# Expert weights spread by DMA, silu in PSUM, and t as the stationary block of the down projection

## The reference

```python
probs = softmax(x @ gate_w)                     # 1024 x 32
w, sel = top_k(probs, 8);  w = w / sum(w)
# an expert takes its first C = 512 tokens, the others are dropped
g = einsum('ech,ehi->eci', xg, w_gate)          # 256 -> 96, each expert
u = einsum('ech,ehi->eci', xg, w_up)
y = einsum('eci,eih->ech', silu(g) * u, w_down) # 96 -> 256
out[token] += w_slot * y
```

## Time and profile before

| | |
|---|---|
| median of 3 runs | 268.94 us (268.77 to 269.79) |
| the profiled execution | 269.13 us |
| its span | 266.8 us |
| mean granted TensorE clock | 0.976 of 2.4 GHz |
| first gate projection starts | 35.8 us |
| second half starts | about 158.6 us |
| last down matmul starts | about 261.0 us |

### The profile page before, as it was taken

The page is one execution under the profiler, slowest core; times in us unless marked ns, Lnnn a source line. Parts: engine busy times, 40 slices in busy tenths (PEclk is TensorE's granted clock), DMA queues, the critical chain, the costliest instruction groups (busy, mean ns, idle before and its releaser), DMA issues.

```text
span 266.8 us, 3968 instructions
## 1 busy us (share of the span) xinstructions
PE 243.9 (91%) x1058; PEld 186.9 (70%) x1061; DVE 134.8 (51%) x342; ACT 134.3 (50%) x242; POOL 161.1 (60%) x140
## 2 busy tenths in 40 slices
PE   6636798799999999999999999999999999999993
PEld 1412486677678777778687778787878787878772
DVE  4598887339562794439643534235342332424333
ACT  2766453576366753594377635343525353435320
POOL 5118202856768565858586675858677686868610
PEclk9999879799999999999999999999999999999998
DMA  7950500006050524124050505050505060700002
GB/s 208 258 147 22 156 26 0 0 0 185 16 154 22 135 64 121 56 50 127 10 169 6 173 1 161 17 153 26 156 21 166 13 173 17 222 22 0 1 0 79
DMA packets 43359, 22.23 MB, mean 83 GB/s; under 512 B 34128, under 2 KB 43344, under 8 KB 43344
## 3 DMA queue, kind: packets, MB, share of 16 engines
q1 hardware_dynamic: 42496, 21.63, 28.1%
q10 hardware_dynamic: 848, 0.43, 0.6%
HBM read 21.01 MB, written 1.05 MB: 83 GB/s over the span
## 4 chain that ended last, share of the span: by engine, by line
PE 68%; DVE 14%; ACT 6%; issue 6%; POOL 4%; DMA 1%; DVEq 0%; POOLq 0%; ACTq 0%
PE bank L699 40%; PE bank L717 8%; PE bank L721 7%; PE bank L718 7%; DVE t_sb L1042 3%; DVE bank L911 2%; DVE inv L922 2%; POOL rstd L357 2%; DVE t_sb L1048 2%; PE bank L616 2%; PE bank L657 2%; PE bank L706 1%; ACT normed L446 1%; DMA x_sb<-in_x_dram 1%; POOL t_lo L375 1%
## 5 line engine op out<-in xcount | busy, mean ns | idle before, releaser
L375 POOL TENSOR_TENSOR t_lo<-t_sb,t_hi 128x512 fp32r<-128x512 f32 x47 | 60.8, 1294 | 75.1 <-ACT t_hi L542 75.1
L349 POOL TENSOR_TENSOR wlo<-raw,whi 128x768 fp32r<-128x768 f32 x48 | 88.5, 1847 | 6.7 <-ACT whi L505 6.5
L699 PE MATMUL bank<-h_hi,whi 128*128 128x512 f32 x192 | 80.8, 421 | 0.3 <-issue 0.3
L1042 DVE TENSOR_TENSOR t_sb<-bank,s_sb 128x512 f32<-128x512 f32 x48 | 33.1, 690 | 93.4 <-PE bank L706 45.8
L699 PE MATMUL bank<-h_lo,whi 128*128 128x512 f32 x192 | 76.7, 400 | 0.0
L699 PE MATMUL bank<-h_hi,wlo 128*128 128x512 f32 x192 | 76.2, 397 | 0.0
L542 ACT ACTIVATE t_hi<-t_sb 128x512 fp32r<-128x512 f32 x48 | 30.3, 630 | 90.9 <-DVE t_sb L1048 90.9
L505 ACT ACTIVATE whi<-raw 128x768 fp32r<-128x768 f32 x48 | 40.0, 835 | 8.6 <-PE bank L721 8.6
L699 PEld LDWEIGHTS bank<-h_hi,whi 128*128 128x128 f32 x192 | 36.9, 192 | 8.8 <-issue 0.8
L699 PEld LDWEIGHTS bank<-h_hi,wlo 128*128 128x128 f32 x192 | 36.6, 191 | 8.8
L699 PEld LDWEIGHTS bank<-h_lo,whi 128*128 128x128 f32 x192 | 36.8, 192 | 8.0
(11 more groups left out here) (120 smaller groups left out, 194.0 us busy)
## 6 DMA issues: line engine op xcount, KB each, us to landing
raw<-in_L_ffn_w_gate_dram SPq DMA_DIRECT2D x16, 384.0 KB
raw<-in_L_ffn_w_up_dram SPq DMA_DIRECT2D x16, 384.0 KB
raw<-in_L_ffn_w_down_dram SPq DMA_DIRECT2D x48, 128.0 KB
out_dram<-x SPq DMA_DIRECT2D x4, 256.0 KB, 2.5
x_sb<-in_x_dram SPq DMA_DIRECT2D x1, 512.0 KB, 7.0
ctx_tile<-in_ctx_dram SPq DMA_DIRECT2D x4, 128.0 KB, 5.2
x_sb<-in_x_dram SPq DMA_DIRECT2D x1, 256.0 KB, 3.4
ctx_sb<-in_ctx_dram SPq DMA_DIRECT2D x1, 256.0 KB, 4.6
```

What stands on the lines that cost most here:

```text
L349: pool.tensor_tensor(split_view(wlo, slot, part), raw_parts(slot, part), split_view(whi, slot, part).bitcast(F32), ALU.subtract).then_inc( ...
L375: pool.tensor_tensor(t_lo[k % 2][:], t_sb[:], t_hi[k % 2][:].bitcast(F32), ALU.subtract).then_inc(t_lo_ready, 1)
L699: last = nc.tensor.matmul(ps[:], up_weight(w, slot, part, k, j), h[:, k, tokens], start=(i == 0), stop=(i == len(terms) - 1))
L1042: nc.vector.tensor_tensor(t1_sb[:], w_ps[:], s_sb[:], ALU.mult).then_inc(t1_ready, 1)
```

## The change

- The routing weights are no longer split into bf16 parts. They are turned as float32 (`turn_chosen`), copied to `route` (32 rows, float32), and for each group SP issues a DMA from SBUF to SBUF (`spread`) that writes the four experts' rows 32 times each into `w_sb[slot]`. DVE waits for its landing (`w_landed`).
- SP's program is written out without loops, with the spreadings in between. The contexts of `later(4)` and `later(5)` are loaded behind reload(4) and reload(6).
- silu is written over g in its PSUM bank; g and u go over a ring of four banks; a projection waits for t1 or t of two steps back.
- In `down`, 128 tokens of t are the stationary block and 256 columns of w_down move: 12 matmuls in place of 6. y comes out with tokens on the partitions, so the copy and the transposes at the end of a half go, and DVE adds straight from the two banks. The first two tiles are signalled (`y_ready`) before the last two.
- Removed: the tables `expert3` and `spread`, `take_y`, `turn_output`, the weights matmul.

```diff
-        ring = (bank[2], bank[3], bank[6])
+        ring = (bank[2], bank[3], bank[6], bank[4])
...
+            def load(n):
+                slot, group = n % 2, n % GROUPS
...
+            def reload(n):
+                sp.wait_ge(w_hi_ready, (n - 1) * 3)
+                sp.wait_ge(w_lo_ready, (n - 1) * 3)
+                load(n)
+            def spread(n):
+                half, group, slot = n // GROUPS, n % GROUPS, n % 2
+                sp.wait_ge(route_ready, ROUTED if half else 2)
+                if n >= 2:
+                    sp.wait_ge(t1_ready, (n - 1) * GT + 1)
+                rows = route[group * EG:(group + 1) * EG, None, half * HALF:(half + 1) * HALF]
+                sp.dma_start(w_sb[slot][:], rows.to_broadcast([EG, QI, HALF])).then_inc(w_landed[slot], 16)
...
+            load(0)
+            load(1)
+            load_context(3)
+            reload(2)
+            spread(0)
+            for n in range(1, 2 * GROUPS):
+                spread(n)
+                if n + 2 < 2 * GROUPS:
+                    reload(n + 2)
+                if n in (2, 4):
+                    load_context(n // 2 + 3)
...
             for u in first_routed:
                 route_exps(u)
+            take_route(first_routed[0])
...
-                nc.scalar.activation(s_sb[:], g_ps(k)[:], ACT.Silu).then_inc(s_ready, 1)
+                nc.scalar.activation(g_ps(k)[:], g_ps(k)[:], ACT.Silu).then_inc(s_ready, 1)
...
-                if part == 0 and (not isinstance(n, int) or n >= 2):
-                    pe.wait_ge(t_ready, n)
-                elif part == 1 and (not isinstance(n, int) or n >= 1):
-                    pe.wait_ge(s_ready, n)
+                if not isinstance(n, int) or n >= 2:
+                    pe.wait_ge((t1_ready, t_ready)[part], n)
...
-                for m in range(KT):
-                    nc.tensor.matmul(y_ps[m][:], down_weight(whi, slot, j, m), t_hi[odd][:], start=False, stop=False)
-                    nc.tensor.matmul(y_ps[m][:], down_weight(wlo, slot, j, m), t_hi[odd][:], start=False, stop=False)
+                def product(t, a, b, stop=False):
+                    return nc.tensor.matmul(y_tile(t), a[odd][:, t * P:(t + 1) * P], down_weight(b, slot, j), start=False, stop=stop)
+                for t in range(HT):
+                    product(t, t_hi, whi)
+                    product(t, t_hi, wlo)
                 pe.wait_ge(t_lo_ready, n + 2)
-                for m in range(KT):
-                    last = nc.tensor.matmul(y_ps[m][:], down_weight(whi, slot, j, m), t_lo[odd][:],
-                                            start=False, stop=last_step)
+                for t in range(HT):
+                    last = product(t, t_lo, whi, last_step and t % NT == NT - 1)
+                    if last_step and t == NT - 1:
+                        last.then_inc(y_ready, 1)
                 last.then_inc(down_done, 1)
...
             project(0, 0, 0, 0, 0, 0)
+            turn_chosen(first_routed[0])
             project(0, 0, 1, 0, 0, 0)
+            turn_chosen(first_routed[1])
             project(1, 0, 0, 0, 1, 0)
-            for u in first_routed:
-                turn_parts(u)
...
-                dve.wait_ge(w_turned, group + 1)
+                dve.wait_ge(w_landed[slot], spreads * 16)
                 dve.wait_ge(s_ready, n + 1)
                 dve.wait_ge(t_ready, n + 1)
-                nc.vector.tensor_tensor(t1_sb[:], w_ps[:], s_sb[:], ALU.mult).then_inc(t1_ready, 1)
+                nc.vector.tensor_tensor(t1_sb[:], g_ps(k)[:], w_sb[slot][:], ALU.mult).then_inc(t1_ready, 1)
...
+                    for t in range(q * NT, (q + 1) * NT):
+                        rows = x1[:, half * HT + t, :]
+                        last = nc.vector.tensor_tensor(rows, rows, y_tile(t), ALU.add)
```

More of the change, by code:

```diff
@@ L161, in program @@
         wlo = [sb(f"wlo{i}", [P, 3, PART], F32R) for i in range(2)]
-        s_sb = sb("s_sb", [P, HALF])
+        w_sb = [sb(f"w_sb{i}", [P, HALF]) for i in range(2)]
         t1_sb = sb("t1_sb", [P, HALF])
@@ L279, in _ @@
             sp.dma_start(x_sb[:, HT:, :], xt[:, HT:, :]).then_inc(x_landed[2], 16)
-            def load(slot, group):
-                experts = bass.ds(group * EG, EG)
+            def load(n):
+                slot, group = n % 2, n % GROUPS
+                experts = slice(group * EG, (group + 1) * EG)
                 for part, w in ((0, wg_dram), (1, wu_dram)):
@@ L287, in load @@
                     sp.dma_start(raw[slot][:, 2, j * C:(j + 1) * C], wd_dram[experts, :, j, :]).then_inc(raw_landed[slot], 16)
-            sp.dma_start(ctx_tile[:], ct[:, HT:HT + 1, :]).then_inc(tile_landed, 16)
-            load(0, 0)
-            load(1, 1)
+            def reload(n):
[9 more added lines that the diff above has]
+                sp.dma_start(w_sb[slot][:], rows.to_broadcast([EG, QI, HALF])).then_inc(w_landed[slot], 16)
             def load_context(n):
                 sp.wait_ge(v_turned, n)
[L295 to L312, removed]
+                sp.dma_start(ctx_tile[:], ct[:, n + 2:n + 3, :]).then_inc(tile_landed, 16)
+            sp.dma_start(ctx_tile[:], ct[:, HT:HT + 1, :]).then_inc(tile_landed, 16)
+            load(0)
[9 more added lines that the diff above has]
+                    load_context(n // 2 + 3)
             for quarter in range(4):
@@ L338, in _ @@
                                pattern=[[1, P]], channel_multiplier=-1)
-            for part in range(3):
-                chain.link(pool.affine_select(out=expert3[:], in_=expert3[:], compare_op=ALU.not_equal, fill=1.0,
-                                              base=-part * E, pattern=[[-1, E]], channel_multiplier=1))
             pool.memset(neg_half[:], -0.5).then_inc(consts_ready, 1)
@@ L572, in turn @@
                         split_high(ahead % 2, k % GT, it * 2 + (half * GROUPS + ahead))
-            def take_y(half):
-                act.wait_ge(down_done, (half + 1) * STEPS + 2)
-                if half:
-                    act.wait_ge(y_turned, 2)
-                for q in range(2):
-                    cols = slice(q * NT * P, (q + 1) * NT * P)
-                    nc.scalar.activation(y_sb[:, 0, cols], y_ps[0][:, cols], ACT.Copy).then_inc(y_copied[0], 1)
             turn(0, 0, later(3), early, early_routed, first_turn=True)
@@ L701, in project @@
                 last.then_inc(ready, 1)
-            def weights(n, half, group):
-                pe.wait_ge(t1_ready, n + 1)
-                nc.tensor.matmul(w_ps[:], spread[:].rearrange("p e i -> p (e i)")[:, bass.ds(group * P, P)],
-                                 route[:, half * HALF:(half + 1) * HALF], start=True, stop=True).then_inc(w_turned, 1)
             def down(n, slot, j, odd, group, last_step=False):
@@ L753, in turn @@
                     if half or not first_turn or k:
-                        project(n, half, 1, slot, j, it * 2 + (half * GROUPS + slot))
-                    if first_turn and k == 0:
-                        pe.wait_ge(route_ready, ROUTED if half else 2)
-                        if half == 0:
-                            pe.wait_ge(tables_ready, 1)
-                    if j == 0:
-                        weights(n, half, it * 2 + slot)
+                        project(n, half, 1, slot, k, it * 2 + (half * GROUPS + slot))
                     if half == 0 and first_turn and k == 0:
@@ L1057, in turn @@
                 for k in range(TURN_STEPS):
-                    step(it * TURN_STEPS + (half * STEPS + k), k, it * 2 + (half * GROUPS + k // GT))
+                    step(it * TURN_STEPS + (half * STEPS + k), k, it + (half * TURNS + 1))
                     for stage, u in beside.get(k, []):
```

135 lines of the change are left out of this document (50 added, 85 removed).

## The result

The changed kernel takes **308.13 us** (median of 4 runs, 307.79 to 309.72), the kernel before 269.37 us beside it (268.77 to 269.84): ratio **1.1452 [1.1402, 1.1502]**. I had forecast 279.0 and a range of 269 to 285: the sign was right, the size was off by 29 us, and the range did not hold it. The profiled execution has a span of 306.6 us, 39.8 more than before. Single executions of one and the same kernel can be slow by one to two per cent: the ratios and their intervals leave these out, the medians count them.

A forecast was written before the change was run, and what follows sets the result against it. TensorE, busy 91% of the span, was taken as the bound. Terms -3.5 + 5.9 + 5.2 + 1.6 + 3.0 - 0.9 - 1.4 = +9.9 us on 269.13 gave 279.0 us, range 269.0 to 285.0.

The forecast's parts named there:

- The first step: Start of step 0: the first spreading lands at 46.0, so t1 starts 3.0 us later, +3.0 us; bounds +1.3 and +5.5.
- The later spreadings: Spreadings of later groups: hidden under a whole group of matmuls while they land in time, so 0 us.
- my bound of 7 us: Upper bound for the first spreading, the longest load's 7 us, which would make the first step +5.5 us.
- more waiting: Rival: two falls of the clock and spreadings late in the groups too, 282 to 290 us; chance 0.12.
- the cover of a group: Second half: a group's matmuls, 12.9 us, hide the later spreading; packets twice as slow would use this up.
- Weights matmul: Steps on TensorE: removing the matmul that makes the routing weights saves 15 x 0.2325, -3.5 us.
- Down: Down projection: 12 matmuls of 256 columns at 0.1265 us replace 6 of 512 at 0.2325, +5.9 us.
- Half price: Rival on down: 256-column matmuls cost half of the 512 price, 0.1165 us, giving 273.2 us; chance 0.14.
- the output: Middle loses 8 transposes on TensorE, -0.9 us; at the end additions start at the half-way signal, -1.4 us.
- Context: Second and third turn: context tile is issued later, so TensorE waits 2.8 and 2.4 us, +5.2; bounds 0 and 8.
- one clock fall: After the two context stalls: TensorE drops once to the 1.2 GHz level, +1.6 us; bounds 0 and +3.2.
- Ring and silu in PSUM: Projections wait on t1 or t of two steps back, and silu reads a PSUM bank: 0 us.

The follow-up runs named there:

- the run with rows 32 apart: Changed kernel with the spreading copying rows 0, 32, 64 and 96 of x, giving wrong weights, on the same four engines: 277.69 us, one run.
- the one with spread rows: Changed kernel with expert 4g + m on partition 8m + g of route, so a group's four rows lie 8 apart: 278.07 us, ratio 1.032.
- the kernel with t as the stationary block alone: Kernel before with only down and the output as changed; weights by matmul and the context's place stay: 268.31 us, ratio 0.9949.
- spread rows and an early context: Changed kernel with a group's rows 8 apart and second and third turn contexts loaded behind reload(3) and reload(5): 266.01 us, ratio 0.9885.

## Why the prediction was wrong

**The step that failed** is the price of the spreading, in "The first step" and, from the same price, "The later spreadings". I had the right four engines, and then gave them the 95 GB/s that four engines had with a source in DRAM. The source here is SBUF, and my bound of 7 us came from loads as well. All that I wrote under "more waiting" on the size of it was that no row shows DMA from SBUF to SBUF, and I gave it 0.12 and 282 to 290 us. I had also written that packets twice as slow would use up the cover of a group. They were four times as slow; the run with rows 32 apart shows that at twice as slow the cover still holds. The runs show the term by itself: 30.1 us between the changed kernel and the one with spread rows, which differ in nothing but the order of the rows of `route` and of the 32 columns that DVE writes for them. By the issues of the spreadings, 14.7 us of the spans' 32.2 lie ahead of that of the second half (178.89 - 42.42 = 136.5 against 164.04 - 42.22 = 121.8), 8.0 of them in the first step (12.48 against 4.49 from the issue to t1), and 14.6 in the six groups from there to 266.40 (87.5 against 72.9).

**What holds, term by term:**
- Weights matmul, -3.5: not run by itself. In the second half a group lasts 12.88 us in the kernel with t as the stationary block alone and 12.72 with spread rows and an early context (by the issues of w_gate); there TensorE is busy all the time in both, so the weights matmul is what differs on it. That is 0.16 a group and not 0.23, some 2.4 us in 15.
- Down, +5.9: too large. The distance is 0.119 us, not 0.1265; 12 x 0.119 - 6 x 0.2325 = +0.033 a step, +1.6 in all. The fixed 0.019 on top of the columns was not right at 256 columns (0.107 + 0.012). "Half price" (0.1165) was the nearest rival. With -0.9 and -1.4 for the output that is -0.7, and -1.1 was measured (-2.1 to -0.6).
- Context, +5.2 and one clock fall, +1.6: the mechanism is right and in the right place, and the kernel before loses about that by it alone (6.6, or 4.0 to 9.2). With spread rows both waits are longer (8.3 us in all, landing 6.2 and 6.4 us after the issue and not 5.0), and the clock falls twice: 12.1. In the changed kernel itself it is 3.7; that the slow spreading takes the rest of its place is likely, not shown.
- First step, +3.0: +11.6, and at least 6.8 us of half clock behind it. This is counted from the first gate projection, which itself varies: 36.13 to 54.90, against 35.78 to 42.99 before. With spread rows it is +3.2 (36.28 to 46.71): at the rate that I had assumed, the rest of this step was right.
- Later spreadings, 0: 14.8 us a group instead of 12.9; 0 with spread rows.
- Ring and silu in PSUM, 0: true for the second half, where TensorE is busy without a gap. In the first half something was put at nothing that is not. Two turns, from w_gate's issue to the next but one, before and with spread rows and an early context:

```profile
73.14:102.22 29.08, 28.01 (x129) 21.71 (x127) 17.68 (x47) 17.42 (x32) 20.31 (x17) 1.00 0.31 86
102.22:131.47 29.25, 28.42 (x130) 22.17 (x130) 17.68 (x47) 17.42 (x32) 20.34 (x17) 1.00 0.28 81
```

```profile
75.30:103.23 27.93, 27.58 (x163) 23.73 (x162) 16.94 (x44) 17.38 (x32) 20.41 (x17) 1.00 0.37 109
103.23:131.18 27.95, 27.60 (x163) 23.75 (x162) 16.96 (x44) 17.38 (x32) 20.42 (x17) 1.00 0.35 103
```

TensorE's idle time in them falls from 1.90 to 0.70 us. The kernel with t as the stationary block alone keeps it (27.78 busy of 28.80), so it comes from the other parts: the ring, silu in PSUM or the shorter making of the weights. No run tells these apart.

Added up with what was measured (-2.4, -1.1, +3.2, -1.2), the kernel with spread rows and an early context should win 1.5 us. Its ratio says 3.1 (1.4 to 4.8), so the account leaves some 1.6 us open, by the interval up to 3.

So two errors nearly cancel with the mended rows (down 4.3 us too dear, context some 5 too cheap), and that its 278.1 us lies so near the forecast of 279.0 is in part luck.

## What to carry to other kernels

A transfer has two ends and the engines between them; here the source end set the rate. For a broadcast out of SBUF, ask which partitions the source rows lie on before counting engines: four rows side by side gave 24 GB/s, the same four experts' rows placed 8 apart about 100, for the price of writing a row of 32 numbers in another order. When an operation is in no row of the trace, its bound has to come from the narrowest thing that it could meet, and not from the slowest transfer of another kind; and the rate at which the cover ends should be turned into a rival with its full time, not left as a remark. In a profile, start-up differs from run to run by more than a small effect (35.14 to 37.49 us to the first gate projection in these), so an early time is best counted from an event of the same trace.

## What the runs showed of the hardware

- DMA engines that are busy for most of the time can move little: 16 engines, mostly at 0.7 to 0.9, with 30 GB/s in all, while they read neighbouring source partitions. The busy share has to be read beside the GB/s.
- The source's partitions set the rate of an SBUF to SBUF transfer at the same engines, packets and bytes: 24, 49 and about 100 GB/s for four neighbours, four rows 32 apart and four rows 8 apart.
- A 128 KB load that is issued right behind transfers on four engines lands after 6.2 and 6.4 us; after 3.7 and 3.2 us when those run on all 16.
- A transfer on the same four engines at 49 GB/s is still covered by a group of matmuls (12.7 us a group); at 24 GB/s it is not (14.8).
- Matmuls with 256 moving columns and a new stationary block each stand 0.119 us apart, where 512 columns take 0.2325.
